# Query projection in the first gather, and the seams of a graph transformer layer

## The reference

```python
xn = layernorm(x)
def gcn(h, W, b):                       # one graph convolution
    msgs = (h @ W)[src] * edge_weight[:, None]
    return segment_sum(msgs, dst) + b
h  = elu(gcn(xn, gW1, gb1)); h = elu(gcn(h, gW2, gb2))
q, k, v = xn @ Wq, xn @ Wk, xn @ Wv     # linear attention, 8 heads
Q, K = elu(q) + 1, elu(k) + 1
KV = einsum('shd,shv->hdv', K, v / L)   # a sum over all nodes
Z  = 1 / (einsum('lhd,hd->lh', Q, K.sum(0)) + 1e-6)
m  = layernorm((einsum('lhd,hdv,lh->lhv', Q, KV, Z) * L) @ Wm, g1, b1)
m  = layernorm(relu(concat([xn, m]) @ W1) @ W2, g2, b2)
x  = x + h + (xn + m)
x  = x + experts(layernorm(x))          # top-1 of 8 experts, with capacity
```

## Time and profile before

| | us |
|---|---|
| median of 3 runs (lowest, highest) | 5139.43 (5133.67, 5143.25) |
| profiled execution, own time | 5136.3 |
| its span in the profile | 5134.5 |
| PE busy / DVE / ACT / POOL | 4113.3 / 2643.0 / 846.1 / 3474.6 |

### The profile page before, as it was taken

The page is one execution under the profiler, slowest core; times in us unless marked ns, Lnnn a source line. Parts: engine busy times, 40 slices in busy tenths (PEclk is TensorE's granted clock), DMA queues, the critical chain, the costliest instruction groups (busy, mean ns, idle before and its releaser), DMA issues. The chain is left out here.

```text
span 5134.5 us, 87736 instructions
## 1 busy us (share of the span) xinstructions
PE 4113.3 (80%) x24996; PEld 3765.1 (73%) x24997; DVE 2643.0 (51%) x9389; ACT 846.1 (16%) x2617; POOL 3474.6 (68%) x3768
## 2 busy tenths in 40 slices
PE   0477777777777777759989898899888998689998
PEld 0476776767766667658888888888888887568887
DVE  7433333333333333345676666666666765554444
ACT  2001000010000000001222222222222221241111
POOL 0577777777777777757777777777777777235554
PEclk9867777777777777658999999999999998599999
DMA  7444444444444444434455545555555455322222
GB/s 212 134 116 119 117 118 118 119 118 118 118 119 118 118 118 119 115 84 118 138 148 148 152 145 146 145 153 146 146 150 150 144 146 152 99 68 76 73 73 69
DMA packets 361208, 639.48 MB, mean 125 GB/s; under 512 B 105581, under 2 KB 230381, under 8 KB 360989
## 3 DMA queue, kind: packets, MB, share of 16 engines
q0 software_dynamic: 171840, 469.16, 32.2%
q1 hardware_dynamic: 181621, 155.12, 9.9%
q10 hardware_dynamic: 7632, 13.77, 0.7%
HBM read 548.73 MB, written 89.00 MB: 124 GB/s over the span
## 5 line engine op out<-in xcount | busy, mean ns | idle before, releaser
L403 PEld LDWEIGHTS sums<-sel,rows 128*128 128x128 f32 x13312 | 1939.0, 227 | 782.7 <-DMA rows<-xn,idx 414.2
L403 PE MATMUL sums<-sel,rows 128*128 128x64 f32 x13312 | 1944.8, 310 | 688.9 <-DMA rows<-xn,idx 312.1
L460 POOL DMA_INDIRECT rows<-xn,idx x1664 | 1577.9, 948 | 644.8 <-issue 634.1
L460 POOL DMA_INDIRECT rows<-h,idx x1664 | 1585.7, 953 | 578.8 <-issue 527.1
L411 DVE TENSOR_SCALAR sel<-cols,rel_now,wgt_now 128x64 f32<-128x64 f32 x3360 | 781.8, 338 | 7.8
L417 DVE TENSOR_TENSOR agg<-agg,sums 128x128 f32 x832 | 240.6, 289 | 786.0 <-issue 570.0
L612 DVE TENSOR_TENSOR pre<-z,b_g 128x256 f32<-128x256 f32 x98 | 41.6, 425 | 558.2 <-PE z L607 558.2
L1816 PE MATMUL e_hidden_ps<-tokens_t,w 128*128 128x256 f32 x1248 | 277.9, 381 | 0.9 <-ACT tokens_t L1840 0.9
L1828 PE MATMUL y_ps<-w,e_hidden 128*128 128x256 f32 x1248 | 277.0, 380 | 0.0
L987 PE MATMUL hidden_ps<-xt,w 128*128 128x128 f32 x1568 | 250.1, 282 | 21.2 <-ACT msg_t L1108 21.0
L1816 PEld LDWEIGHTS e_hidden_ps<-tokens_t,w 128*128 128x128 f32 x1248 | 238.5, 191 | 34.1 <-ACT tokens_t L1840 1.3
(11 more groups left out here) (227 smaller groups left out, 4701.9 us busy)
## 6 DMA issues: line engine op xcount, KB each, us to landing
rows<-xn,idx POOLq DMA_INDIRECT x1664
rows<-h,idx POOLq DMA_INDIRECT x1664
w<-in_ffn_w SPq DMA_DIRECT2D x16, 1024.0 KB, 7.8
ln_rows<-in_x SPq DMA_DIRECT2D x52, 256.0 KB
xn<-ln_normed ACTq DMA_DIRECT2D x52, 256.0 KB, 4.4
kv_tile<-xn SPq DMA_DIRECT2D x98, 128.0 KB, 2.2
h<-h_rows SPq DMA_DIRECT2D x98, 128.0 KB, 2.1
tile<-xn SPq DMA_DIRECT2D x98, 128.0 KB
```

The lines of the kernel that those rows point to most:

```text
L403: last = nc.tensor.matmul(sums[:, g, h, :], rows[:, u, k, h * P:(h + 1) * P], sel[:, u, k, :], start=(c == 0), stop=(c == GROUP - 1))
L460: nc.gpsimd.indirect_dma_start(out=rows[:, u, k, :], out_offset=None, in_=source, in_offset=bass.IndirectOffsetOnAxis(ap=idx[:, u, k:k + 1 ...
```

## The change

In prepare ScalarE makes the normalised rows, as rows x scale + shift, and VectorE only the scale and the shift (`scale`). Seven blocks are in flight, 49 blocks are normalised instead of 52, and the rest of `xn` is zeroed by one DMA at the start. The spans come behind the first seven blocks, the tables ahead of the last seven. GpSimd loads the edge weights and zeroes `agg` for the first gather. The other constants are loaded by SP in the first gather, ahead of `w_g` and `b_g`, and scaled by VectorE at its end, where the kv block's work now stands too (`dve_close`). The first two turns' indices are loaded ahead of each gather, into a buffer both share.

The query projection with its elu moves from `attend` to `keys_values`, which has the transposed tile already. Transposed tile and queries are stored to DRAM (`store`) and loaded again by the second gather (`load`, `load_more`).

```diff
-PSLOTS = 4
+PSLOTS = 7
...
+                for u in range(2):
+                    sp.dma_start(m.idx[:, u, :], m.in_src[u]).then_inc(m.idx_first, 16)
+                sp.wait_ge(m.idx_first, 32)
 
             @block.scalar
             def _(act):
-                def store(i, s):
+                def normalise(i, s, first):
+                    wait_apart(act, rstd_done, 2 * (i * PSLOTS + s + 1), m.act_passed)
+                    if not first:
+                        act.wait_ge(xn_stored[s], 16 * i)
+                    for j in range(PB):
+                        last = nc.scalar.activation(normed[:, s, j, :], rows[:, s, j, :], ACT.Identity,
+                                                    scale=rstd[:, s, j:j + 1], bias=shift[:, s, j:j + 1])
+                    last.then_inc(xn_done, 1)
...
+                act.preload_act_table_set("sqrt_and_others")
                 act.wait_ge(zero_set, 1)
-
-                act.dma_start(m.xn[NP:NP + P, :], m.zeros[:, 0:D]).then_inc(pad_stored, 16)
+                tiles = (NP - UNITS * P) // P + 1
+                act.dma_start(m.xn[UNITS * P:NP + P, :].rearrange("(t p) f -> p t f", p=P),
+                              m.zeros[:, 0:D].rearrange("p (o f) -> p o f", o=1).to_broadcast([P, tiles, D])
+                              ).then_inc(pad_stored, 16)
+                act.wait_ge(eps_set, 1)
...
+                pool.dma_start(m.wgt[:, 0:NCH], m.in_wgt).then_inc(wgt_loaded, 16)
...
+                nc.gpsimd.memset(m.agg[:, :, :], 0.0).then_inc(agg_zeroed, 1)
...
+                def scale(i, s):
+                    dve.wait_ge(sd_done, i * PSLOTS + (s + 1))
+                    nc.vector.reciprocal(rstd[:, s, :], sd[:, s, :]).then_inc(rstd_done, 1)
+                    dve.wait_ge(rstd_done, 2 * (i * PSLOTS + s) + 1)
+                    nc.vector.scalar_tensor_tensor(shift[:, s, :], mv[:, s, :, 0], -1.0, rstd[:, s, :],
+                                                   ALU.mult, ALU.mult).then_inc(rstd_done, 1)
...
+                turn(0, True)
                 dve.wait_ge(edges_loaded, 32)
...
-                turn(0, True)
-                turn(1, False)
-                with dve.Fori(2, loops) as i:
+                with dve.Fori(1, loops - 1) as i:
                     turn(i, False)
...
+                dve.wait_ge(wgt_loaded, 16)
                 nc.vector.memset(m.wgt[:, NCH:NCH + SLOTS], 0.0).then_inc(tables_done, 1)
-                dve.wait_ge(consts_loaded, 16 * len(consts))
-                nc.vector.tensor_scalar(m.ln1_gh[:, :], m.ln1_gh[:, :], -0.5, None, ALU.mult).then_inc(tables_done, 1)
-                nc.vector.tensor_scalar(m.ln2_gh[:, :], m.ln2_gh[:, :], -0.5, None, ALU.mult).then_inc(tables_done, 1)
-                nc.vector.tensor_scalar(m.ln2_b[:, :], m.ln2_b[:, :], -1.0, None, ALU.add).then_inc(tables_done, 1)
+                turn(loops - 1, False)
+                scale(loops - 1, PSLOTS - 1)
+                wait_apart(dve, agg_zeroed, 1, m.passed)
                 wait_apart(dve, early_ready, 2, m.passed)
-                dve.wait_ge(tables_done, 15)
+                dve.wait_ge(tables_done, 12)
...
                 for u in range(2):
-                    sp.dma_start(idx[:, u, :], m.in_src[u]).then_inc(idx_loaded[u], 16)
                     mix.load(sp, u, u)
+                    mix.load_more(sp, 0, u)
                 mix.load_weights(sp)
                 dense.load_weights(sp)
...
+                    if has_tile(i, u):
+                        mix.load_more(sp, i, u)
...
+                if layer == 1:
+                    for u in range(2):
+                        sp.wait_ge(rows_loaded[u][BANKS - 1], 16 * GROUP * SUB * loops)
+                        sp.dma_start(idx[:, u, :], m.in_src[u]).then_inc(m.idx_first, 16)
                 for u in range(2):
                     dense.sp(sp, loops - 1, u)
+                mix.stored(sp)
...
+                pool.wait_ge(m.idx_first, 32 * layer)
+                turn(0)
+                wait_apart(pool, rows_used[1], 1, m.pool_passed)
+                turn(1)
+                with pool.Fori(1, loops) as i:
                     for u in range(2):
...
+                        ready(i, u)
+                        turn(u)
...
-                nc.vector.memset(m.agg[:, :, :], 0.0).then_inc(agg_zeroed, 1)
+                take(0, 0)
+                if layer == 2:
+                    nc.vector.memset(m.agg[:, :, :], 0.0).then_inc(agg_zeroed, 1)
                 mix.dve_begin(dve)
                 dense.dve_begin(dve)
-                take(0, 0)
-                dve.wait_ge(agg_zeroed, 1)
+                if layer == 2:
+                    dve.wait_ge(agg_zeroed, 1)
...
+                mix.dve_close(dve)
...
+        for to, of in consts:
+            sp.dma_start(to, of).then_inc(consts_loaded, 16)
...
+        if place == 2:
+            if not before_first(i, u, 1):
+                wait_apart(pe, queries_ready, t, m.pe_passed)
+            for h in range(KD):
+                for k in range(KD):
+                    last = nc.tensor.matmul(query_ps[:, h, :], w_q[:, k, h * P:(h + 1) * P], xt[:, u, k, :],
+                                            start=(k == 0), stop=(k == KD - 1))
+            last.then_inc(query_projected, 1)
...
+            dve.wait_ge(query_projected, t + 1)
+            nc.vector.tensor_scalar(q_min[:, :, :], query_ps[:, :, :], 0.0, None, ALU.min).then_inc(q_min_ready, 1)
+        if place == 3:
+            if not before_first(i, u, 2):
+                wait_apart(dve, q_stored[u], 32 * i, m.passed)
+            dve.wait_ge(q_exp_ready, t + 1)
+
+            nc.vector.scalar_tensor_tensor(queries[:, u, :, :], query_ps[:, :, :], 0.0, q_min[:, :, :],
+                                           ALU.max, ALU.add).then_inc(queries_ready, 1)
...
+        if not before_first(i, u, 2):
+            wait_apart(act, q_stored[u], 32 * i, m.act_passed)
...
+    def exp_query(act, i, u, place):
+        if place == 2 and has_tile(i, u):
+            act.wait_ge(q_min_ready, 2 * i + (u + 1))
+            nc.scalar.activation(q_min[:, :, :], q_min[:, :, :], ACT.Exp).then_inc(q_exp_ready, 1)
...
+    def store(sp, i, u):
+        t = 2 * i + u
+        sp.wait_ge(xt_ready, t + 1)
+        sp.dma_start(m.xt[bass.ds(t * P, P), :], xt[:, u, :, :].rearrange("p k n -> p (k n)")).then_inc(q_stored[u], 16)
+        sp.wait_ge(queries_ready, t + 1)
+        sp.dma_start(m.qt[bass.ds(t * P, P), :], queries[:, u, :, :].rearrange("p k n -> p (k n)")
+                     ).then_inc(q_stored[u], 16)
+
...
+        sp.dma_start(queries[:, u, :, :], m.qt[bass.ds(t * P, P), :].rearrange("p (k n) -> p k n", k=KD)
+                     ).then_inc(queries_loaded[u], 16)
+
+    def load_more(sp, i, u):
+
+        if not before_first(i, u, 2):
+            sp.wait_ge(hidden_done, 2 * i + (u - 1))
+        t = 2 * i + u
+        sp.dma_start(xt[:, u, :, :], m.xt[bass.ds(t * P, P), :].rearrange("p (k n) -> p k n", k=KD)
+                     ).then_inc(xt_loaded[u], 16)
...
-                pe.wait_ge(queries_ready, t + 1)
+                wait_apart(pe, queries_loaded[u], 16 * i + 16, m.pe_passed)
                 for h in range(KD):
-                    last = nc.tensor.matmul(num_ps[:, h, :], queries[:, h, :], m.kv[:, h, :], start=True, stop=True)
+                    last = nc.tensor.matmul(num_ps[:, h, :], queries[:, u, h, :], m.kv[:, h, :], start=True, stop=True)
...
-            if has_tile(i, u, 1):
-                turn_tile(pe, t + 1, 1 - u, i + u)
...
-            if has_tile(i, u, 1):
-                project_queries(pe, t + 1, 1 - u)
+            wait_apart(pe, xt_loaded[u], 16 * i + 16, m.pe_passed)
...
-        if place == 0 and has_tile(i, u):
-            dve.wait_ge(q_exp_ready, t + 1)
-
-            nc.vector.scalar_tensor_tensor(queries[:, :, :], query_ps[:, :, :], 0.0, q_min[:, :, :],
-                                           ALU.max, ALU.add).then_inc(queries_ready, 1)
...
-        prepare(nc, m)
+        m.idx = sb("idx", [P, 2, SLOTS], I32)
+        m.idx_first = ctx.enter_context(nc.semaphore("idx_first"))
         with ExitStack() as agg_ctx:
             m.agg = agg_ctx.enter_context(nc.sbuf_tensor("agg", [P, KD, AGG], F32))
+            prepare(nc, m)
```

More of the change, by code:

```diff
@@ L213, in store, with turn @@
                                   normed[:, s, :, :]).then_inc(xn_stored[s], 16)
-                act.wait_ge(eps_set, 1)
-                with act.Fori(0, loops) as i:
+                def turn(i, first):
                     for s in range(PSLOTS):
@@ L259, in _, with statistics, turn @@
                 nc.vector.memset(m.eps[:, :], LN_EPS).then_inc(eps_set, 1)
+                def statistics(i, s):
+                    dve.wait_ge(x_loaded[s], 16 * i + 16)
+                    for j in range(PB):
+                        last = nc.vector.bn_stats(stats[:, s, j, :], rows[:, s, j, :])
+                    last.then_inc(stats_done, 1)
```

(33 more changed lines are left out.)

172 lines of the change are left out of this document (75 added, 97 removed).

## The result

The changed kernel takes 5492.63 us in the median (5477.99 to 5527.82, 4 runs) against 5136.65 (5133.67 to 5143.25): ratio 1.0701, 95% interval [1.0649, 1.0753]. It is slower by 7%, where I forecast 5066 us and faster.

| stage | before | forecast | after |
|---|---|---|---|
| first row asked for at | 151.1 | 123.5 | 123.9 |
| first gather, first to last row | 2092.7 | 2086.7 | 2103.0 |
| seam, last to first row | 32.1 | 28.6 | 28.3 |
| second gather, first to last row | 2132.1 | 2096.3 | 2495.9 |
| rest | 726.6 | 726.6 | 725.2 |

A forecast was written before the change was run, and what follows sets the result against it. GpSimd's gather issue, 1.25 us a row, was taken to bound both gathers. Gains of 27.6 + 6 + 3.5 + 6.3 + 29.5 = 72.9 from 5136.3 gave 5063.4, written as 5066 us for the median; range 5036 to 5112.

The forecast's parts named there:

- Prepare: Stage before the gathers: ScalarE takes 2.0 us a block, first row at 123.5 against 151.1, -27.6 us.
- First gather, start and turns: First gather: selection ahead of zeroing gives -6 us with a stall of 3 left; the added work each turn costs 0.
- rival C: First gather becomes TensorE's: turns of 20.55 us, 54 more, 5120 us; chance 0.06 given back in part, 0.04 in full.
- One sign that I gave: First gather: TensorE's waits for rows down to 1 to 2 us a turn.
- Seam: Between the gathers, last sum to first row: indices already loaded and one block boundary gone, -3.5 us (-1 to -6).
- Second gather, turns: Second gather: 1.25 us leave VectorE's chain each turn, GpSimd alone is then the bound, -29.5 us (0 to -35.6).
- rival B: Second gather keeps its stalls, as TensorE sets its turn or gets a lower clock: 29.5 back, 5096 us; chance 0.13.
- Second gather, start: Start of the second gather: GpSimd's stalls of 12.9 us become one of 6.6, -6.3 us (0 to -12.9).
- GpSimd's pitch: Both gathers: GpSimd issues a gather instruction every 1.25 us, the floor; a move of it would prove the forecast wrong.

The follow-up runs named there:

- the seams alone: The changed kernel with the query projection left in the second gather as before, plus 60 semaphore increments ahead of VectorE's second loop: 5119.92 us, ratio to before 0.9966.
- 36 increments: The changed kernel with 36 semaphore increments that nothing waits for, added once ahead of VectorE's second-gather loop: 5117.12 us, ratio to before 0.9949.
- the table on ScalarE's queue: The changed kernel with 36 increments and the edge-weight table loaded on ScalarE's queue instead of GpSimd's: 5085.95 us, and 5075.4 us when timed again.

## Why the prediction was wrong, by its steps

- **Prepare, right.** First row at 123.9 for 123.5. I had the size for partly wrong reasons: ScalarE's pair takes 1.08 us, not 1.04, and ScalarE did stand, 24.9 us for VectorE's variances. The estimate of 1.08 by the formula of the Trainium skill's page "ScalarE: Activation LUTs", section "What ACT_TABLE_LOAD costs", was right at 256 columns; at 128 the same formula gives an estimated 0.86 where the earlier trace rows show 0.81, so there the trace agreed less well than I wrote. The wait:

```profile
ACT ln_sd L214 <- DVE ln_mean_var L273: 24.9, 20, 12.2
```

- **First gather, start and turns, right.** No stall at the start (I left 3), and the 784 added matmul passes cost nothing: the 16 us more are about what the pitch takes. TensorE's busy time is even that of before, 1570.8 for 1569.9: it is granted 0.76 of its clock for 0.73. In the run with the seams alone it is 1586.4 at 0.72, so with more matmuls it has the better clock here, as I argued against rival C. One sign that I gave failed: its waits for rows did not go down to 1 to 2 us a turn but up, from 293.5 to 457.3 in all, 4.7 a turn, while those for VectorE's sum fell from 179.7 to 24.9. Why was not tested.
- **Seam, right:** -3.8 for -3.5.
- **Second gather, turns: the step that failed.** "1.25 less brings the turn below GpSimd's 20.0. Then GpSimd alone is the bound and most of the 35.6 goes". I counted VectorE's operations and forgot that an instruction has to be there to run. With the loop one piece of code too long VectorE loses 4.15 and 2.08 us a pass, TensorE waits for the selection, and -29.5 became +364; moving the code alone gives 373 back (2122.4 for 2495.9). A pass grows by 10.2 us in the median (50.85 against 40.64 with 36 increments), some 4 more than the stalls. TensorE's clock falls with them: it stood 4.94 us for VectorE's message, and meanwhile the granted clock fell to 0.50, 1.2 GHz, where it stayed until 3572 us; then it was 1.00, 2.4 GHz. The 16 products of a group take 3.5 us at the one level and 1.9 at the other (the windows as above, and TensorE's timeline):

```profile
3552.00:3572.00 20.00, 16.86 (x69) 15.34 (x70) 11.55 (x45) 3.16 (x12) 10.17 (x11) 0.50 0.48 137
3573.00:3602.00 29.00, 22.84 (x177) 21.42 (x176) 13.79 (x54) 5.16 (x16) 20.86 (x22) 1.00 0.48 134
```

```profile
3553.35 0.69 PE L1036 MATMUL turn_ps<-ident,msg 128*128 128x128 f32 x2 [4.94 <-DVE msg L1103]
...
3563.09 3.51 PE L400 MATMUL sums<-sel,rows 128*128 128x64 f32 x16
...
3577.57 1.89 PE L400 MATMUL sums<-sel,rows 128*128 128x64 f32 x16
```

  That the clock makes up those 4 us was not tested by itself. None of my rivals had the code; rival B had a lower clock, but bounded by the old pace, and the gather took 364 us longer than that.
- **The same step's size.** With the code in place, what the move brings can be read from two runs on one chip: 5111.47 (5110.31 to 5112.14) with it, 5119.92 (5110.98 to 5122.64) without, second gather 2130.1 for 2138.3. So VectorE's chain was worth some 8 us at the slower pitch, not 29.5, and as the ranges overlap even that is not clear of noise. At the old pitch no run has the seams alone. Without its stalls at the start the second gather took 2119.2 us before and, with all changes, 2110.3 and 2098.2 in the two runs with the table on ScalarE's queue: 9 to 21 us less.
- **Second gather, start, mis-sized:** a stall of 12.74 instead of 6.6. The zeroing of the sums started 8.6 us behind the first row (2263.81), not 4, for VectorE stands 5.13 us ahead of it. It had stood 6.42 there in the first gather before, which I did not count.

```profile
2263.81 21.07 DVE L491 MEMSET agg<- 128x25216 f32 x1 [5.13 <-DMA b_g<-in_gnn_b]
```

  The releaser named is doubtful: in the run with 36 increments the same 5.13 us are put down to "issue".
- **GpSimd's pitch.** I named 1.25 as the floor and its move as what would prove me wrong. It moved to 1.261, 17 us on 1663 steps, for a load that I had counted only among the bytes of the prepare stage. The first gather paid it in full. The second paid 7 in one pair of profiles (2129.8 against 2122.9) and 17 in another (2127.5 against 2110.4), and nothing in the kernel before.

## What to carry to other kernels

A loop's time can hang on where its code lies: when a change adds or removes instructions ahead of a long loop, compare the packets of the code queues, and look for "issue" time behind the branch and inside straight code. Some idle instructions ahead of the loop test it in one run. And where an engine's issue is the bound, look what its queue carries besides: one load on it, at a time when the engine had nothing else to do, cost the first gather 18 us here.

## What the runs showed of the hardware that I had not expected

- In these runs VectorE kept a loop that lies in three pieces of 8 KB of code, as counted; with a fourth it fetched five packets a pass and stood 3.4 to 4.2 us at the head, and 2.1 to 2.4 more at the next piece where that began three or seven instructions behind the head.
- With one load of 832 KB on GpSimd's queue (171,984 packets in place of 171,840) each of 3328 later gather instructions took about 10 ns longer; a second such load added nothing.
